# Moving layer-norm work between queues in a block of adaLN attention and a block-scaled FFN

## The reference

```python
def reference(L0_attn_x, ..., L0_c, L0_wmod):
    ...
    x = L0_attn_x
    mod = (_silu(L0_c) @ L0_wmod).reshape(L0_c.shape[0], 6, 1, -1)
    sa, ca, ga, sb, cb, gb = (mod[:, 0], mod[:, 1], mod[:, 2], mod[:, 3], mod[:, 4], mod[:, 5])
    ga = (2 * (ga >= 0) - 1) * jnp.maximum(jnp.abs(ga), 0.25)
    gb = (2 * (gb >= 0) - 1) * jnp.maximum(jnp.abs(gb), 0.25)
    h = _layernorm(x, axis=-1) * (1 + ca) + sa
    x = x + ga * _L0_attn_ref(h, L0_attn_Wq, ..., L0_attn_bo)
    h = _layernorm(x, axis=-1) * (1 + cb) + sb
    x = x + gb * _L0_ffn_ref(h, L0_ffn_weight, L0_ffn_bias)
    return x
```

## Time and profile before

| what | us |
|---|---|
| median of three runs | 288.09 (285.27 to 288.89) |
| the profiled execution, device time | 287.7 |
| its span, first to last instruction | 285.8 |
| mean granted TensorE clock in it | 0.974 of full |

### The profile page before, as it was taken

How to read it: one execution, slowest core, us unless ns; L and a number is a source line. 1 busy time by engine, 2 the same in 40 slices (tenths; PEclk the granted TensorE clock), 3 DMA queues, 4 the chain that set the end, 5 groups by cost and what they waited for, 6 DMA issues and landing times.

```text
span 285.8 us, 4279 instructions
## 1 busy us (share of the span) xinstructions
PE 247.6 (87%) x1296; PEld 154.7 (54%) x1296; DVE 258.7 (91%) x326; ACT 210.5 (74%) x567; POOL 211.2 (74%) x153
## 2 busy tenths in 40 slices
PE   6999988597969796889979997999898988996885
PEld 1653554166514651466546743674357745894664
DVE  3699799969995999999999998899999999999980
ACT  2386987965797778879895989987686666676743
POOL 7201439895879999999999997999999699945200
PEclk9999999999989997999988999999998899999999
DMA  7753977694785149714993489126952865740006
GB/s 231 177 189 80 342 244 238 225 337 149 210 283 160 61 141 359 230 65 134 362 309 79 128 295 323 65 52 210 361 189 76 258 193 172 232 146 14 0 0 220
DMA packets 54385, 53.88 MB, mean 189 GB/s; under 512 B 4094, under 2 KB 52812, under 8 KB 54364
## 3 DMA queue, kind: packets, MB, share of 16 engines
q1 hardware_dynamic: 54364, 53.63, 59.0%
HBM read 44.89 MB, written 8.72 MB: 188 GB/s over the span
## 4 chain that ended last, share of the span: by engine, by line
DVE 39%; POOL 17%; ACT 15%; PE 13%; issue 12%; DMA 1%; DVEq 0%; POOLq 0%; ACTq 0%
POOL pv_buf L677 13%; DVE prod L1718 9%; DVE pv_buf L1848 9%; DVE prod L1848 4%; DVE prod L1707 3%; PE ps L1070 2%; ACT dump L1200 2%; PE ps L857 2%; PE ps L839 2%; ACT dump L1191 2%; ACT dump L1241 1%; DVE ps L1822 1%; DMA x_in<-in_L_attn_x 1%; PE ps L828 1%; ACT hT L1266 1%
## 5 line engine op out<-in xcount | busy, mean ns | idle before, releaser
L677 POOL TENSOR_TENSOR pv_buf<-pv_buf 128x1024 f32<-128x1024 f32 (+2 forms) x60 | 132.5, 2208 | 15.0 <-DVE pv_buf L1848 9.7
L1718 DVE TENSOR_TENSOR prod<-ps,kT 128x1024 f32<-128x1024 f32 (+4 forms) x70 | 75.1, 1109 | 0.0
L1848 DVE TENSOR_TENSOR pv_buf<-v_shift,ps 128x1024 f32<-128x1024 f32 x49 | 59.1, 1211 | 0.0
L941 PE MATMUL ps<-prod,sel_sum 128*32 128x512 f32 x256 | 33.0, 635 | 8.7 <-DVE prod L1718 8.2
L839 PE MATMUL ps<-hT,wT 128*128 128x512 f32 x64 | 30.7, 621 | 0.0
L857 PE MATMUL ps<-wT,h_cen 128*128 128x256 f32 x128 | 29.9, 379 | 0.0
L828 PE MATMUL ps<-hT,wT 128*128 128x512 f32 x64 | 29.6, 595 | 0.3 <-ACT hT L1266 0.2
L991 PE MATMUL ps<-wo_g,w_raw 128*128 128x256 f32 x112 | 28.1, 396 | 0.0
L857 PEld LDWEIGHTS ps<-wT,h_cen 128*128 128x128 f32 x128 | 23.9, 190 | 6.4 <-issue 3.8
L991 PEld LDWEIGHTS ps<-wo_g,w_raw 128*128 128x128 f32 x112 | 22.3, 199 | 4.0 <-issue 0.2
L941 PEld LDWEIGHTS ps<-prod,sel_sum 128*32 128x32 f32 x256 | 6.9, 112 | 28.9 <-DVE prod L1718 13.8
(11 more groups left out here) (213 smaller groups left out, 538.5 us busy)
## 6 DMA issues: line engine op xcount, KB each, us to landing
v_shift<-v_rows SPq DMA_DIRECT2D x56, 512.0 KB, 5.9
x_in<-in_L_attn_x SPq DMA_DIRECT2D x8, 512.0 KB, 4.3
v_rows<-v_base SPq DMA_DIRECT2D x8, 512.0 KB, 4.1
x_res<-in_L_attn_x SPq DMA_DIRECT2D x8, 512.0 KB, 6.1
out_x<-outb SPq DMA_DIRECT2D x5, 512.0 KB, 5.2
rows_mod<-mod_rows SPq DMA_DIRECT2D x7, 256.0 KB, 3.4
x<-in_L_wmod SPq DMA_DIRECT2D x1, 1024.0 KB, 8.3
row_ga<-mod_rows SPq DMA_DIRECT2D x8, 128.0 KB, 5.0
```

The lines of the kernel that those rows point to most:

```text
L677: nc.gpsimd.tensor_tensor(dst, dst, ring(b, n)[:, t:NT, :], ALU.add).then_inc(s_add, 1)
L941: mm = nc.tensor.matmul(ps23[32 * g:32 * g + 32, 1, :], sel_sum[:, which, c, :], prod[:, n, c, :], start=(c == 0 and which == 0), stop=(c ...
L1718: nc.vector.tensor_tensor(prod[:, n, :, o:L], ps01[:, :, o:L], kT[:, b % 2, :, 0:L - o], ALU.mult).then_inc(s_prod, 1)
L1848: nc.vector.tensor_tensor(dst[:, t:NT, :].rearrange("p t (h e) -> p t h e", e=DH), v_n.rearrange("p t (h e) -> p t h e", e=DH), weights, A ...
```

## The change

ScalarE: `norm_before` moves from the end of an iteration behind the next one's `exps`; `squares_after(b-1)` moves from the end of iteration b to the head of iteration b+1 (there as `squares_after(b-2)`), `quantised(b-3)` forward to behind it, and `norm_after(b-2)` back from behind `exps` to behind `evacuate_attention(b-1)`. Iteration 5 keeps the old place for sequence 4 as well. GpSimd: `rstd_both` is replaced by `rstd_after(b-2)` at the head and `rstd_before(b+3)` after add 5; `modulate` and `gate_ffn` come behind add 1, `gate_projection` behind add 9. SyncE's loads of the gate and modulation rows follow. TensorE turns the first four blocks of the scores when the first copy is there.

```diff
--- before.py
+++ after.py
@@ -304,7 +304,7 @@
             return 0 <= i < B
 
         def rstd2_ready(b, half_=None):
-            return (s_rs1, NRS1 * (b + 5)) if has(b + 4) else (s_rs2, NRS2 * (upto_half(b, half_) - TAIL))
+            return s_rs2, NRS2 * upto_half(b, half_)
 
         def upto(i):
             return min(max(i, 0), B)
@@ -508,10 +508,8 @@
             for b in range(LAST - 1):
                 if has(b + 3):
                     load_x(b + 3)
-                if has(b - 2):
-                    load_rows_mod(b - 1)
-                if has(b - 3):
-                    load_row_gb(b - 2)
+                if b > 0:
+                    load_row_ga(b)
                 spill_v(b + 1)
                 shift_v(b + 1, 1)
                 shift_v(b + 1, 2)
@@ -527,7 +525,10 @@
                     load_bias_att(0)
                     load_bias_ffn(0)
                 shift_v(b + 1, 4)
-                load_row_ga(b + 1)
+                if has(b - 2):
+                    load_rows_mod(b - 1)
+                if has(b - 3):
+                    load_row_gb(b - 2)
                 shift_v(b + 1, 5)
                 shift_v(b + 1, 6)
                 if has(b - 3):
@@ -537,6 +538,7 @@
                     store(b - 3)
             load_bias_ffn(LAST - 3)
             spill_v(LAST)
+            load_row_ga(LAST - 1)
             load_rows_mod(LAST - 2)
             load_row_gb(LAST - 3)
             shift_v(LAST, 1)
@@ -650,21 +652,12 @@
                 pool.wait_ge(s_rs1, NRS1 * b + 1)
                 nc.gpsimd.tensor_tensor(shift1[:, :], negmean1[:, :], rstd1[:, :], ALU.mult).then_inc(s_rs1, 1)
 
-            def rstd_both(b):
-
-                pool.wait_ge(s_var1, b + 4)
-                pool.wait_ge(s_xnorm, b + 3)
-                pool.wait_ge(s_var2, b)
-                nc.gpsimd.tensor_tensor(rstd[:, :], var[:, :], minus_half[:, :], ALU.pow).then_inc(s_rs1, 1)
-                pool.wait_ge(s_rs1, NRS1 * (b + 3) + 1)
-                nc.gpsimd.tensor_tensor(shift[:, :], negmean[:, :], rstd[:, :], ALU.mult).then_inc(s_rs1, 1)
-
             def rstd_after(b, half_=None):
 
                 t, _, _ = halves(half_)
                 pool.wait_ge(s_var2, upto_half(b, half_))
                 nc.gpsimd.tensor_tensor(rstd2[:, t], var2[:, t], minus_half[:, t], ALU.pow).then_inc(s_rs2, 1)
-                pool.wait_ge(s_rs2, NRS2 * (upto_half(b, half_) - TAIL) - 1)
+                pool.wait_ge(s_rs2, NRS2 * upto_half(b, half_) - 1)
                 nc.gpsimd.tensor_tensor(shift2[:, t], negmean2[:, t], rstd2[:, t], ALU.mult).then_inc(s_rs2, 1)
 
             def add(b, n):
@@ -699,27 +692,27 @@
             split_gated_biases()
             for b in range(LAST - 1):
                 if has(b - 2):
+                    rstd_after(b - 2)
+                if b == 0:
+                    rstd_before(2)
+                add(b, 1)
+                if has(b - 2):
                     modulate(pool, nc.gpsimd, b - 2)
                 if has(b - 3):
                     gate_ffn(b - 3)
-                if b == 0:
-                    rstd_before(2)
-                add(b, 1)
                 add(b, 2)
                 add(b, 3)
                 add(b, 4)
-                gate_projection(b)
                 add(b, 5)
+                if has(b + 3):
+                    rstd_before(b + 3)
+                else:
+                    rstd_after(b - 1)
                 add(b, 6)
-                if has(b + 3) and has(b - 1):
-                    rstd_both(b)
-                elif has(b + 3):
-                    rstd_before(b + 3)
-                elif has(b - 1):
-                    rstd_after(b - 1)
                 add(b, 7)
                 add(b, 8)
                 add(b, 9)
+                gate_projection(b)
             modulate(pool, nc.gpsimd, LAST - 3)
             gate_ffn(LAST - 4)
             add(LAST - 1, 1)
@@ -958,13 +951,15 @@
                     mm.then_inc(s_sp, 1)
 
             def scores_by_token(b):
-                pe.wait_ge(s_s, 2 * b + 2)
+                pe.wait_ge(s_s, 2 * b + (1 if b < LAST else 2))
                 ps = ps67 if b < LAST else ps23
                 if b < LAST:
                     x_free(b)
                 for t in range(NT):
                     col = TCOL * (t % 2)
                     nc.tensor.transpose(ps[:, t // 2, col:col + P], s_sb[:, P * t:P * t + P], ident[:, :])
+                if b < LAST:
+                    pe.wait_ge(s_s, 2 * b + 2)
                 for t in range(NT):
                     col = TCOL * (t % 2) + P
                     mm = nc.tensor.transpose(ps[:, t // 2, col:col + P], s2_sb[:, P * t:P * t + P], fold[:, :])
@@ -1472,16 +1467,20 @@
                     evacuate_k(1, 0)
                     sums_before(2)
                     squares_before(2)
-                if has(b - 2) and has(b + 2):
-                    norm_after(b - 2)
+                elif ahead:
+                    norm_before(b + 2)
+                if has(b - 2):
+                    squares_after(b - 2)
+                if has(b - 3):
+                    quantised(b - 3)
                 evacuate_v(b + 1, 1)
                 if b == 0:
                     norm_before(2)
                     evacuate_v(b + 1, 0)
                 else:
                     evacuate_attention(b - 1)
-                if has(b - 3):
-                    quantised(b - 3)
+                if has(b - 2):
+                    norm_after(b - 2)
                 if ahead:
                     h_modulated(b + 2, 1)
                     h_modulated(b + 2, 0)
@@ -1507,18 +1506,16 @@
                     squares_before(b + 3)
                 if b == 1:
                     evacuate_weight(4)
-                if has(b - 1):
+                if not norm1:
                     squares_after(b - 1)
                 if has(b - 3):
                     take_result(b - 3, 0)
                     take_result(b - 3, 1)
 
                 copy_scores(b + 1)
-                if has(b + 2):
+                if ahead:
                     seed_q(b + 2)
-                if has(b + 3):
-                    norm_before(b + 3)
-                elif has(b - 1):
+                if not norm1:
                     norm_after(b - 1)
 
             quantised(LAST - 4)
```

## The result

| | us |
|---|---|
| changed kernel, median of four runs | 297.4 (297.27 to 297.7) |
| before, median of four runs | 287.6 (285.27 to 288.89) |
| ratio, 95% interval | 1.035 (1.028 to 1.042) |
| profiled execution, span, granted clock | 297.33, 295.6, 0.971 |

Runs over 1.5% above the fastest of their kernel are left out of all ratios.

What follows compares the result with a forecast made beforehand. VectorE (29.77 us list) and GpSimd (29.6) were both taken as full. Iteration changes of -3.15, -0.15, +1.8, -0.05, +1.95 and +2.1 summed to +2.5 us on 287.7: 290.2 us, range 283.5 to 294.5.

Steps and rivals of the forecast that it cites:

- Exponentials and T2: VectorE's exponential waits shrink 1.98 and 1.55 us in iterations 1 and 2; the 1.17 us score wait starting iteration 2 goes.
- Scores in two parts: Turning scores on TensorE in two parts can give at most part of VectorE's 3.4 us wait; value taken 0.
- Two roots: Two roots on GpSimd instead of one double root add 0.65 us to its list in each of iterations 2 to 4.
- the ring: Slack between GpSimd's additions and VectorE's products, said to hide GpSimd's lateness at first, until p9 waits for add 5.
- The new loop: Add 9, transposes, evacuations, norm_after, modulate, additions: a 31.7 us closed way through four engines, GpSimd idle 1.4 us per iteration.
- The term 6.4 us: Time from the end of add 9 through transposes, evacuations and copies to the end of norm_after: 6.4 us.
- Iteration 6: VectorE waits for h2, 2.1 us late because GpSimd starts modulate(4) later; iteration takes 32.3 us (+2.1).
- The step that failed: TensorE's wait before the transposes of attention grows from 1.03 us to some 2.2.
- T: Start of softmax_max on VectorE in each iteration, numbered by iteration; the forecast counted its times from there.
- rival B: TensorE's clock falls behind longer waits before attention's transposes, about 1.6 us in each of iterations 2 to 5: 296.6; chance 0.10.

Runs made afterwards that it cites:

- fillers of the right length: Changed kernel with 2, 4, 2 and 3 overwritten fp32 matmuls over all 128 rows on TensorE before its wait for add 9, iterations 2 to 5: 293.4 us.
- long fillers: Changed kernel with 4, 9, 5 and 6 overwritten fp32 matmuls over all 128 rows on TensorE before its wait for add 9, iterations 2 to 5: 300.7 us.

## Why the prediction was wrong

- *Exponentials and T2*: right. Iteration 1 took 26.29 us for 26.2; the exponentials by themselves gave 2.9 us where their two waits were 3.5, and T2's wait then grew to 2.46 us.
- *Scores in two parts*: right at 0: in the changed kernel VectorE nowhere waits for the scores. On the kernel before the 0 is in part luck, as a fall of the clock came with it and took back what T2 gained.
- *Two roots*: right in length (1.02 and 0.20 us, twice). On the kernel before they cost 1.9 us, more than the ring was thought to let through, by a way that stays open; in the changed kernel the loop hides whether they cost more.
- *The new loop*: the mechanism was right and is shown: reordering two neighbours on GpSimd gives 7.5 us back. The term 6.4 us was 6.8 in iteration 4: 0.2 lie between the end of add 9 and the transposes (157.61 to 157.79), another 0.2 behind them.
- *Iteration 6*: right, 2.06 us for 2.1.
- *The step that failed* is TensorE's wait before the transposes, "which grows from 1.03 us to some 2.2", and with it the full clock that the loop's 6.4 us took for granted. I counted from T, as if TensorE began q_rows when VectorE began softmax_max. Once GpSimd holds VectorE at its last products, the scores are turned ahead of time, and q_rows begin ahead of T, 3.5 us in iteration 3 and 0.7 in iteration 5: TensorE waited 1.95, 5.67, 2.14 and 2.90 us. After 5.67 and 2.90 the clock was at half, in the middle of the loop. This is rival B's mechanism at its place, and it got 0.10. B had it in four iterations at 1.6 us; it came in two, which ended 2.8 and 2.5 us late. GpSimd's waits there are 2.6 and 1.7 us longer than the 1.96 of the other two iterations, so that the clock's part is about 4.3 us of the 7.1 that the forecast missed; the fillers of the right length give 4 back.
- *The range* followed from that: it ended at 294.5, "short of most of B".
- *The page cited beside B*, the Trainium skill, "TensorE: Matmul & The Clock Gate", Part 1, says that idling brings the array to half rate. The traces agree in part: in the changed kernel the clock fell after 2.90 and 5.67 us and held after 1.95 and 2.14. That a wait of some 2.2 us would bring a cold start in each iteration, as the prediction drew from it, is not what the page says, and it did not come out: two iterations fell. The length of the wait alone doesn't tell: in the runs above the clock held after 3.06 us (two roots, iteration 2) and fell after 2.29 (fillers of the right length, iteration 1). The thing to do was to work out the wait on TensorE's own queue before giving B its chance.

The 7.1 us are so: 5.3 in iterations 3 and 5 (4.3 the clock, 0.2 and 0.8 the rest), 1.0 in 2 and 4 (29.53 for 28.9, 32.13 for 31.75), 0.2 in 1 and 6, 0.9 before T1 and behind T7, less 0.2 outside of the span (rounded terms). The 0.8 of iteration 5 and the 0.9 have no cause that I can show; single runs of one kernel differ by as much.

## What to carry to other kernels

When two engines are nearly full, don't price an edit by the length of a queue alone: draw the closed way that work takes through the engines from one iteration to the next, and check which queue idles in it; putting one ready addition into that idle time was worth 7.5 us here. Work out each engine's wait on its own queue: an engine that isn't the bound can run ahead and take its slack in one wait, as TensorE did with 5.67 us, and such a wait can cost its clock right where the loop needs it. Look at the clock of every execution, too: one profiled execution need not be the typical one, as modulate behind add 2 showed by 3 us. Split a change of many edits: the one edit that paid gave 1.0% by itself, and the rest took 4.5% away.

## What the runs showed of the hardware

Fillers of nine bf16 matmuls on 3 of 128 rows did not hold TensorE's clock each time: behind 2.1 us of them without a gap, v_rows took 3.23 us for 1.89 in iteration 4; in iteration 5, with a gap of 0.78 us behind the same fillers, they took 1.89. Behind fp32 matmuls over all rows v_rows took 1.89 us in each of iterations 2 to 5 (1.9 us of them and a gap of 0.4 us, for example). Whether it is the rows or the type that counts wasn't tried.

How long TensorE idled did not alone decide its clock. At the same place, before the fillers of iteration 3, it idled 2.39 us in the run of the long fillers and 2.40 in that of the right ones; eighteen records then took 7.96 us, at full clock, and eight took 5.37, where they take 3.60 at full clock.

One fp32 matmul of 128x512 shows as two records of 0.43 us each, and counting one for the whole cost one experiment.
